# First attention stage: one activation table set for Exp and Ln, and two steps reordered

## What is computed

```python
x = x + _L0_attn_ref(_layernorm(x), w, w_out)

def _L0_attn_ref(x, w, w_out):          # 16 heads of L = 8
    q, k, v = jnp.split(jnp.matmul(x, w.T), 3, axis=2)
    k_exp = jnp.exp(k * scale) + 1e-06
    k_norm = jnp.cumsum(k_exp, axis=0)  # over the tokens
    qs = jax.nn.softmax(q * scale, axis=-1) / k_norm
    # carry += k_t v_t^T ;  y_t = qs_t carry   (a scan over the tokens)
    ...
    return jnp.matmul(y, w_out)
```

## Time and profile before

| what | value |
|---|---|
| median of 3 runs | 722.83 us (721.58 to 724.45) |
| the profiled execution | 724.99 us, of which the span from first to last instruction is 723.2 us |
| busy over the span | PE 605.6, DVE 528.2, ACT 395.3, POOL 378.0 us |
| first attention stage | about 16 to 178 us of the span |
| one steady turn (start of `qe` to start of the next, five times) | 17.0 us |
| mean granted TensorE clock | 0.952 |

### The profile page before, as it was taken

The page is one execution under the profiler, slowest core; times in us unless marked ns, Lnnn a source line. Parts: engine busy times, 40 slices in busy tenths (PEclk is TensorE's granted clock), DMA queues, the critical chain, the costliest instruction groups (busy, mean ns, idle before and its releaser), DMA issues.

```text
span 723.2 us, 14496 instructions
## 1 busy us (share of the span) xinstructions
PE 605.6 (84%) x4148; PEld 363.9 (50%) x4148; DVE 528.2 (73%) x1869; ACT 395.3 (55%) x826; POOL 378.0 (52%) x537
## 2 busy tenths in 40 slices
PE   2778999994009999999987888899999999998994
PEld 1445556653005778777765344445454545453543
DVE  3478888896962454464679799798989898987554
ACT  2466556533703222245322567877777777767882
POOL 0388888881027777758745643343343434333341
PEclk9999999998557999999999899999999999999997
DMA  9930000000401223424632440312022121100111
GB/s 294 268 64 1 2 1 0 0 0 1 145 15 52 49 46 59 83 64 71 100 56 27 78 67 4 47 25 49 22 38 35 31 41 27 44 3 3 32 57 31
DMA packets 44522, 36.72 MB, mean 51 GB/s; under 512 B 4192, under 2 KB 39568, under 8 KB 44448
## 3 DMA queue, kind: packets, MB, share of 16 engines
q1 hardware_dynamic: 34112, 27.83, 16.6%
q0 software_dynamic: 8992, 7.38, 7.0%
q10 hardware_dynamic: 1344, 0.62, 0.3%
HBM read 13.93 MB, written 8.91 MB: 32 GB/s over the span
## 4 chain that ended last, share of the span: by engine, by line
PE 40%; DVE 18%; issue 10%; POOL 6%; ACT 3%; DMA 1%; DVEq 0%; ACTq 0%; POOLq 0%
DVE rows_home L1787 9%; PE bank L2173 8%; PE wide L2160 5%; PE wide L1315 5%; PE bank L1323 5%; PE bank L2095 4%; POOL x_dram L1046 4%; POOL x_row L1038 2%; PE wide L1333 2%; PE wide L2095 2%; PE bank L2185 2%; DVE st L301 1%; DVE slot_t L878 1%; ACT L276 1%; DVE slot_v L876 1%
## 5 line engine op out<-in xcount | busy, mean ns | idle before, releaser
L1950 ACT ACTIVATE pexp<-wide 128x512 f32<-128x512 f32 (+2 forms) x384 | 181.4, 537 | 75.8 <-PE wide L2160 73.8
L1880 POOL TENSOR_SCALAR_AFFINE_SELECT pexp<-pexp 128x256 f32<-128x256 f32 x256 | 105.8, 417 | 169.6 <-ACT pexp L1950 167.9
L1787 DVE CUSTOM_DVE_ANT_0 rows_home<-bank,mask_qk 128x384 f32<-128x384 f32 (+3 forms) x326 | 142.0, 482 | 11.7 <-PE bank L2095 10.7
L2160 PE MATMUL wide<-qT,kTe 128*128 128x256 bf16 (+3 forms) x512 | 121.9, 302 | 4.7 <-ACT pexp L1950 2.2
L1298 ACT ACTIVATE hT<-wide,b1T 128x512 f32<-128x512 f32 x64 | 43.8, 686 | 131.0 <-PE wide L1315 129.9
L1787 DVE CUSTOM_DVE_ANT_0 rows_home<-wide,mask_qk 128x512 f32<-128x512 f32 (+3 forms) x186 | 86.8, 493 | 25.4 <-PE wide L2095 25.2
L1046 POOL DMA_INDIRECT x_dram<-yg,row_u x48 | 76.2, 1588 | 36.0 <-DVE yg L1096 23.5
L2095 PE MATMUL bank<-kTm,qT 128*128 128x384 bf16 (+3 forms) x326 | 78.9, 304 | 14.6 <-DVE rows_home L1787 11.4
L1038 POOL DMA_INDIRECT x_row<-xln_dram,row_u x64 | 62.5, 977 | 52.6 <-DVE slot_tok L907 33.4
L2173 PE MATMUL bank<-pexp,vx 128*32 128x512 f32 (+3 forms) x1024 | 83.9, 439 | 0.5 <-POOL pexp L1880 0.5
L1315 PE MATMUL wide<-xgT,w_sb 128*128 128x512 f32 x128 | 68.8, 626 | 1.6 <-DVE xgT L1078 1.6
(11 more groups left out here) (279 smaller groups left out, 975.6 us busy)
## 6 DMA issues: line engine op xcount, KB each, us to landing
qT<-rows_home SPq DMA_DIRECT2D x144, 64.0 KB
qT<-kTm SPq DMA_DIRECT2D x3, 1024.0 KB, 14.8
x_sb<-in_L_attn_x SPq DMA_DIRECT2D x8, 256.0 KB, 7.5
w_sb<-in_L_ffn_w SPq DMA_DIRECT2D x1, 2048.0 KB, 13.4
xln_dram<-rows_home SPq DMA_DIRECT2D x8, 256.0 KB, 2.2
out_x<-x_sb SPq DMA_DIRECT2D x7, 256.0 KB, 2.3
x_dram<-x_sb SPq DMA_DIRECT2D x6, 256.0 KB, 2.7
x_sb<-x_dram SPq DMA_DIRECT2D x6, 256.0 KB, 4.1
```

Of the source, the lines that this page charges most:

```text
L1787: ins = nc.vector.tensor_tensor_reduce(out=masked[:, n % 4, at], in0=bank_of(n)[:, at], in1=mask_qk[:, T - w:T], scale=1.0, scalar=LEAST, ...
L1880: nc.gpsimd.affine_select(out=pexp[:, at, :, 0:P], in_=pexp[:, at, :, 0:P], pattern=[[0, 2], [1, P]], compare_op=ALU.is_ge, fill=0.0, base ...
L1950: nc.scalar.activation(pexp[:, exp_slot(b, 2 * step + h // 2), h % 2:h % 2 + nh, 0:w], scores_bank(b, m)[:, 0:nh * w].rearrange("p (h t) - ...
L2160: ins = nc.tensor.matmul(scores_bank(b, m)[:, hh * w:(hh + 1) * w], kTe[:, par, j * P:(j + 1) * P], qT[:, b % QB, 4 * qd + h + hh, j * P:T ...
```

## The change

The Ln preset behind `qe` goes (in each turn and ahead of the stage). The two presets that loaded the Exp set (ahead of the stage, and behind the square root between turns 0 and 1) become a load of a set that is named outright and that holds both Ln and Exp. On ACT `xln(b+2)` comes ahead of `qe(b+1)` in each turn. On DVE `stats(b-2)` comes ahead of `qmax(b+1)`.

```diff
@@ dve_lin_turn
             dve_lin_reduce(dve, b, 0)
+            if before:
+                dve_lin_stats(dve, b - 2)
             if front:
                 dve_lin_qmax(dve, b + 1, 1 - par)
-            if before:
-                dve_lin_stats(dve, b - 2)
             dve_lin_prod(dve, b, 1)
@@ act_lin_turn
-            if front:
-                act_lin_qe(act, b + 1)
-                act_preset(act, ACT.Ln)
             if front and ahead:
                 act_lin_xln(act, b + 2)
             if front:
+                act_lin_qe(act, b + 1)
                 act_lin_seed(act, b + 1)
@@ lin_act
             act_lin_qe(act, 0)
-            act_preset(act, ACT.Ln)
             act_lin_xln(act, 1)
...
             act_std(act, B // 2, B, "ln1_second")
-            act_preset(act, ACT.Exp)
+            nc.scalar.preload_act_table_set("natural_log_exp_and_others")
             act_lin_turn(act, 1, 1)
```

## The result

The changed kernel took 716.47 us (median of 4 runs, 714.81 to 717.87) against 723.61 us for the kernel before (4 runs, 721.58 to 724.45): a ratio of 0.9916, 95% interval 0.9893 to 0.9939, so 0.6 to 1.1% faster. The forecast was 716.1 us. The profiled execution of the changed kernel has a span of 716.1 us, 7.1 less than before.

A forecast was written before the change was run, and what follows sets the result against it. The ring `qe`, seed, `qw`, `shift` through ACT and POOL was taken to set the 17.0 us turn. Front 2.9 + turns 3.8 = 6.7 us, from 722.83 to 716.1 us; range 713.5 to 719.7.

The forecast's parts named there:

- The ring: First attention stage: `qe`, seed, `qw`, `shift`, next `qe` through ACT and POOL sets the 17.0 us turn.
- Turns 2 to 5: Steady turns of the first attention stage: PE's waits for `tT` vanish, saving 3.8 us in all.
- a turn shortens by PE's own wait for `tT`: Turns 2 to 5: each saves only PE's wait ahead of its transposes, 0.97, 1.12, 0.55 and 1.13 us.
- The front: Ahead of turn 0 and turn 0 into turn 1: without the loads, PE's `qkv` moves 2.9 us earlier.
- PE's `states` end 2.0 earlier: Turn 0 into turn 1: PE's `states` end at 48.8 instead of 50.83.
- the clock's risk: Stage's last turn and PE's restart after it: lower clock may shift, about 0.9 us either way; no change taken.
- the sign that I named for the front: Profile after: the front is right if `xT` of sequence 2 starts near 52.3.
- the loads carry the gain in the turns: Steady turns: removing two 1.28 us loads brings the gain; moving `xln` ahead of `qe` is costed at nothing.
- The slower rival: Turns 0 to 5 and ahead: named set not held, both loads in the seed, 3.5 us lost, 726.3 us; chance 0.04.
- `stats` ahead of `qmax`: DVE in the turns: the new order costs nothing and brings nothing that PE lets through.
- The late `qmax`: Turns 2 to 5: `shift` waits for `qmax`, some 2.5 us given back, 718.6 us; chance 0.20 with smaller hand-over losses.
- Turns 6 and 7, and what follows: Stage's last turns, without transposes for a later sequence, give nothing; what follows is the same program begun earlier.

The follow-up runs named there:

- e8: Kernel before plus four extra 128x128 matmuls on PE in each sequence's yT step; 725.86 us against 722.27, ratio 1.0041.
- e9: Changed kernel plus four extra 128x128 matmuls on PE in each sequence's yT step; 723.05 us against the changed kernel's 716.47 and 716.21 in other jobs.
- e5: The changed kernel measured once more, nothing altered, against the kernel before; 716.21 us, ratio 0.9928.
- e1: Kernel before with the named table set alone, `xln` and `stats` not moved; 716.62 us, ratio 0.9922.
- e2: Kernel before with `xln` ahead of `qe` alone, both table loads and the Ln preset kept; 716.12 us, ratio 0.9920.
- e4: Changed kernel with Exp and Ln loaded by function again, no Ln preset, both reorderings kept; 718.13 us, ratio 0.9937 to the kernel before.
- e3: Kernel before with `stats` ahead of `qmax` on DVE alone; 722.02 us, ratio 0.9988.
- e7: Changed kernel plus 12 and 9 extra matmuls of constants where PE idles ahead of turn 0 and in it; 714.76 us, ratio 0.9888 to the kernel before.

## Why the prediction was right, point by point

**The ring: right, and shown.** `qe`, seed, `qw`, `shift` set the turn before; PE sets it after (e8, e9). The next bound was named before it was seen, and the turns came out at 15.9 to 16.1 us (forecast 16.0 to 16.3).

**Turns 2 to 5: 3.8 us forecast, 4.1 measured.** The rule "a turn shortens by PE's own wait for `tT`" held within 0.05 us in turns 2, 3 and 5: 1.00, 1.08 and 1.09 us against the 0.97, 1.12 and 1.13 of the earlier trace rows. Turn 4 gave 0.95 against a marked wait of 0.55. The mark understates the wait: from `states` to the transposes of turn 4 the starts lay 121.02 - 119.63 = 1.39 us apart before and 115.91 - 115.24 = 0.67 after, so 0.72 us came from that place. By the same marks it was 1.13, 1.28 and 1.29 us in turns 2, 3 and 5, about 0.16 above the mark in each turn. Those three lost 0.13 to 0.20 us of it elsewhere, so that they match the marks to 0.05 us is in part luck.

```profile
119.63 0.83 PE L711 MATMUL wide<-qv,kx 128*128 128x128 f32 x6
```

```profile
115.24 0.83 PE L708 MATMUL wide<-qv,kx 128*128 128x128 f32 x6
```

In turn 4 the other 0.23 us came from between the transposes just ahead of it and its first running sums (starts 0.79 us apart before, 0.56 after). That is where the hardware loop starts over; why it shrank is not shown. e8 agrees that turn 4 had more room than its mark: it took in 0.89 us of extra work there and stayed at 17.09 us.

**The front: 2.9 us forecast, 1.8 in the first profile, 2.8 in e5's** (39.51 against 36.67 us from `qe` of sequence 0 to the transposes of turn 1). The step itself was right: Exp ended 2.1 us earlier relative to `qe` (33.46 + 0.63 - 30.09 = 4.00, against 6.11 by the earlier trace rows). The step that fell short is "PE's `states` end 2.0 earlier": counted from `qe` of sequence 0 they ended 0.7 us earlier in the first profile and 1.7 in e5's. What I did not see is that PE, idle 2.29 us ahead of the key sums of sequence 1, could then meet a lower clock in turn 0; it took 1 us back in the first profile and nothing in e5's. I had put the clock's risk in the last turn and behind the stage only. So the sign that I named for the front failed in the first profile, where `xT` of sequence 2 started at 53.35 and not near 52.3. The two ends of the stretch in e5:

```profile
28.73 0.63 ACT L519 ACTIVATE qe<-q_sh 128x512 f32<-128x512 f32 x1 [3.64 <-POOL q_sh L608]
```

```profile
65.40 0.60 PE L677 MATMUL bank<-cst,xln 128*128 128x128 f32 x4
```

**Which part carries what: half wrong.** I said that the loads carry the gain in the turns and that moving `xln` is worth nothing. The first half holds for the change as a whole, since e1 alone gives all of it. But e2 gives the same turns with both loads in place. The failing step was to price `xln` only behind the removal of the loads ("behind `qe` it would cost nothing either"). Priced alone, it lets Ln start as soon as `den` is there, and `qe` to the end of Exp falls from 6.10 to 5.0 to 5.25 us, which is enough to reach PE's rhythm. Two edits that shorten one ring are not added: the first to reach the next bound takes all.

**The slower rival: its price was wrong.** It did not come about: the named set was held through the loop. And it would not have been slower: the load for Ln does not wait with its ACTIVATE (e4), so it hides behind DVE's `qsum` and `den`, and e4 took 718.13 us where the rival had 726.3. The step that failed is the sum 117.2 + 1.28 + 0.57 + 1.28 + 0.63, in which the first 1.28 does not belong.

**`stats` ahead of `qmax`: right.** It brings nothing, alone (e3) or with the rest (e1 has the other order and the same turns). The late `qmax` did not become the ring: it ends at 107.18, and `shift` begins at 108.47.

**Turns 6 and 7, and what follows: 0 forecast, right but for the clock.** The 1.42 us of the first table were the clock of one profile (e3). The sum came out 0.4 us short of the first medians and 1.1 us above the second (721.83 - 716.21 = 5.6 us), with run-to-run spreads of about 3 to 6 us in either kernel. That the two profiles differ by 7.1 us, so near to 6.7, is partly luck: 1.42 us of clock in the last turn made up for the 1.1 us that the front fell short.

## What to carry to other kernels

Follow the ring, not the busy share: here the idlest engine held the turn, and 10.8 us on POOL plus 6.1 on ACT made the 17.0. Once it is found, look for the wait that the ring imposes on the next fullest engine; that wait, turn by turn, was nearly the whole gain of the turns. And price each edit by itself as well as with the others, because a second edit on the same ring may find nothing left.

## What the runs showed of the hardware

In e4 a table load on ACT did not wait for what its ACTIVATE waited for: it started at 111.78, right behind `qe`, while the ACTIVATE that needed it started at 113.86 behind a wait for DVE, and so in every turn of that run. A preset was not needed to hide that load there. Ahead of turn 0, where `xln` stands between `qe` and Ln, the load came behind `xln` in e4 (31.19), and `qe` to the end of Exp took 6.02 us, against 6.11 with the preset in the kernel before. Whether this is the engine's doing or that of the place where the program puts the load, the traces do not say.

The lower of PE's two clocks (granted 0.50, 1.2 GHz) came in the front after idle times of 2.3 to 3.3 us, but not in every execution: 2.39 us of idling left the clock at 1.00 in the profile of before, the same 2.39 us in e1 were followed by 0.50 over 42 to 44 us, and 2.29 us in the changed kernel by 0.57 over 43 to 47 us. Matmuls without a purpose in those idle times kept it at 1.00 (e7). Such stretches moved the time of one execution by about 1 us (turn 0: 23.26 against 22.25 us) to 1.7 us (last turn: 37.73 against 36.07), as much as some of the effects looked for here; the gap between two fixed marks inside the affected stretch told the cases apart where the total could not.
